# Layers 1 to 3 of a graph network: ring slots freed by counted steps, tile stores issued by ScalarE, words read as 16-bit halves

## The chip, the cores and the metric

The kernel runs on 1 core of one Trainium2 chip. The metric is the device time of one execution in microseconds (us), of the core's whole program. The number to compare against is the median of 3 runs of the kernel before.

## The reference

Four layers of a graph network run over 6250 nodes with 256 features each and 100,000 edges. The edges are sorted by destination node. Each layer ends in `x = layernorm(x + layer(x))`. What matters of it:

```python
edge_index = jnp.stack([src, dst])
x = _layernorm(x + _L0_gnn_ref(x, edge_index, ...))            # attention, 8 heads, softmax over a node's edges
x = _layernorm(x + _L1_gnn_ref(x, edge_index, ...))            # two graph convolutions:
    # msg = h[src] * norm[:, None]; segment_sum(msg, dst) + b;  256 -> 512 -> 256, layer norms and relu
x = _layernorm(x + _L2_gnn_ref(x, edge_weight, W, b, src, dst))
    # msg = hw[src] * sym_norm[:, None]; relu(segment_sum(msg, dst) + b)
x = _layernorm(x + _L3_gnn_ref(x, edge_index, edge_attr_2, ...))  # mixed messages, 4 heads, softmax weights
```

In every layer the costly part is the same: for each edge, fetch the row of its source node, scale it, and add it to the sum of its destination node.

## The kernel before

**Chunks, tiles, steps.** The nodes lie in 49 tiles of 128 (`T = NODE_TILES`), the edges in chunks of 128. A pass over the edges gathers 783 chunks (`POSITIONS`): GpSimd issues one indirect DMA a chunk, which brings 128 rows of 256 numbers from a table in HBM into a slot of a ring in SBUF (`ring_rows`, 60 slots, `SLOTS`). A chunk on the border of two tiles is used for both, so there are 831 steps (`RANKED`), and step i uses chunk i minus the rank of its tile (0 to 48). The rank, the ring slot and the number of chunks that must have landed are data: they are worked out at the start and stored in `step_rows`. `slot_row` has one 32-bit word a step: the slot's offset in the low half, the chunks needed in the high half. `ends_row` has one word a chunk: how many steps must be over before the chunk's slot is free.

**Stages.** A start and layer 0 (with its own loop), then three passes by the class `EdgePass` (line 1372 on): pass 1 and pass 2 are the two convolutions of layer 1 (`edges1`, `edges2`), pass 3 is layer 2 (`edges3`). The change's words count these as "layers 1 to 3". The last stage is layer 3 of the reference, called `mix_...` here and layer 4 in the text. A stage's gathers read a table that the stage before stores tile by tile, so GpSimd begins a pass only when all 49 stores have landed.

**A step of a pass.** TensorE multiplies a one-hot matrix (which edge goes to which node, made by ScalarE in `hots`, or with weights by VectorE in `weighted_hots`) by the gathered rows (`step`, line 1453); VectorE adds the product to the tile's sum in `reg_acc` (`add`, line 1463). When a tile's last step is over, its closing runs spread over the next 16 steps (`closings`, `PARTS`): in pass 1 dense layer, layer norm, second dense layer, at the end ScalarE's scaled copy out of PSUM (line 1533; lines 1670 and 1783 in passes 2 and 3).

**What sets the order.** Each engine's queue is written out by hand, and the engines meet at semaphores:
- GpSimd (`EdgePass.gpsimd`, line 1399) waits ahead of gather j until the product of step j - 12 is made (`AHEAD = SLOTS - (NODE_TILES - 1)` is 12). As step j - 12 uses chunk j - 12 - rank, this is 12 + rank chunks.
- SP (`EdgePass.sync`) waits for the arrival of each chunk in order and counts it on one semaphore, `landed` (line 1414), on which TensorE waits. Between two arrivals, at the chunks that `STORE_AT` names, it waits for a closed tile's copy and issues the store of that tile (line 1410).
- Ahead of pass 2, SP issues the loads of the layer's weights and, by `load_x` (line 463), seven loads of 896 KB that bring `x` back. All of this stands ahead of `EdgePass.sync` in SP's queue.
- TensorE reads the slot words into registers, 16 steps at a time (`load_slots`, line 846), and takes each apart with a mask (line 850) and a shift (in `chunks_needed`). ScalarE and VectorE do the same in layer 4.
- In layer 4 (`mix_gpsimd`, `mix_sync`) GpSimd may be 60 chunks ahead already: SP reads `ends_row` (`load_ends`, line 865), waits until that many steps are over, and signals the slot free (line 1875), 8 chunks early (`FREE_EARLY`).

Of the kernel before, what the change touches and what calls it, by code (L numbers as in the profile page):

```python
# [8 lines left out]
I32 = mybir.dt.int32  # L9
ALU = mybir.AluOpType  # L10
# [6 lines left out]
FEAT = 256  # L17
# [27 lines left out]
AHEAD = SLOTS - (NODE_TILES - 1)  # L45
# [20 lines left out]
STORE_AT = [min(WHOLE[k] + PARTS + 3 - k, POSITIONS) for k in range(T)]  # L66
# [193 lines left out]
def build(nc, io):  # L260
    ctx = ExitStack()
    with ctx:
# [26 lines left out]
        ends_row = step_rows[ROW_OF_ENDS:ROW_OF_ENDS + 1, 0:POSITIONS]  # L289
        group_row = sb("group_row", NODE_TILES, rows=1)  # L290
# [39 lines left out]
        s_landed = [signal(f"pass{k}_landed") for k in (1, 2, 3, 4)]  # L330
        s_free = signal("slot_free")
# [508 lines left out]
        def load_slots(e, name, t0):  # L840

            if name not in slot_regs:
                slot_regs[name] = ([e.alloc_register(f"slot{k}") for k in range(GROUP)],
                                   [e.alloc_register(f"part{k}") for k in range(2)])
            n = min(GROUP, STEPS_PAD - t0)
            e.load(slot_regs[name][0][0:n], slot_row[:, t0:t0 + n])

        def slot_rows(e, name, t, a, b):
            words, parts = slot_regs[name]
            e.reg_alu(parts[0], words[t % GROUP], PLACES - 1, op=ALU.bitwise_and)  # L850
            v = e.snap(parts[0], min_val=0, max_val=(SLOTS - 1) * FEAT)
            return scratch[:, bass.DynSlice(v + a if a else v, b - a)]

        def chunks_needed(e, name, t):
            words, parts = slot_regs[name]
            e.reg_alu(parts[1], words[t % GROUP], 16, op=ALU.logical_shift_right)
            return e.snap(parts[1], min_val=1, max_val=POSITIONS)
# [3 lines left out]
        def load_ends(e, c0, n):  # L861

            if not end_regs:
                end_regs.extend(e.alloc_register(f"end{k}") for k in range(ENDS_AT_ONCE))
            e.load(end_regs[0:n], ends_row[0:1, c0:c0 + n])  # L865
# [511 lines left out]
        class EdgePass:  # L1377
# [6 lines left out]
            def __init__(self, table, weighted, landed, banks):  # L1384
                self.table, self.weighted, self.banks = table, weighted, banks
                self.landed = landed
                self.landed_n = landed.take(POSITIONS)
                self.got = [s_slot[k].take(len(range(k, POSITIONS, ARRIVALS))) for k in range(ARRIVALS)]
                self.product, self.added = s_edge.take(RANKED), s_added.take(RANKED)
                if weighted:  # L1390
                    self.hot = s_hot.take(RANKED)
                else:
                    self.far, self.hot4 = s_far.take(RANKED), s_hot4.take(-(-RANKED // 4))

            def gpsimd(self, e):
                for j in range(POSITIONS):
                    if j >= AHEAD:
                        e.wait_ge(*self.product(j - AHEAD))
                    e.indirect_dma_start(  # L1399
                        ring_rows[:, j % SLOTS, :], None, self.table,  # L1400
                        bass.IndirectOffsetOnAxis(ap=src_idx[:, j:j + 1], axis=0)).then_inc(*self.got[j % ARRIVALS].up)

            def sync(self, e, table, taken, stored, at):


                done = 0
                for j in range(POSITIONS + 1):
                    while done < T and STORE_AT[done] == j:
                        e.wait_ge(*taken(done))
                        e.dma_start(node_rows(table, done, done + 1), at(done)).then_inc(*stored[done % len(stored)].up)  # L1410
                        done += 1
                    if j < POSITIONS:
                        e.wait_ge(*self.got[j % ARRIVALS](j // ARRIVALS))
                        e.sem_inc(*self.landed_n.up)  # L1414
# [60 lines left out]
        edges1 = EdgePass(tab_x1, False, s_landed[0], psum[6:8])  # L1475
# [39 lines left out]
        def pass1_scalar(e):  # L1515
            edges1.hots(e, range(8))
            for i in range(RANKED + PARTS):
                edges1.hots_ahead(e, i)
                for k, n in closings(i):
# [11 lines left out]
                    if n == 16:  # L1531
                        e.wait_ge(*dense2.product(k))
                        e.mul(sums[:, k, :], dense2.out(k), dinv[:, k:k + 1]).then_inc(*taken2.up)

# [30 lines left out]
        def close1_sync(e):  # L1565
            edges1.sync(e, tab_h2, taken2, [h2_stored], lambda k: acc[:, k:k + 1, 0:FEAT])
# [12 lines left out]
        edges2 = EdgePass(tab_h2, False, s_landed[1], psum[4:8])  # L1579
# [13 lines left out]
        def pass2_sync(e):  # L1593
# [9 lines left out]
            edges2.sync(e, tab_x2, taken_l2, x2_stored, lambda k: staged[:, k % 2:k % 2 + 1, :])  # L1603
# [41 lines left out]
        def pass2_scalar(e):  # L1645
            edges2.hots(e, range(8))
            for i in range(RANKED + PARTS):
                edges2.hots_ahead(e, i)
                for k, n in closings(i):
# [16 lines left out]
                    if n == 16:  # L1666
# [3 lines left out]
                        e.copy(staged[:, k % 2, :], dense_l2.out(k)).then_inc(*taken_l2.up)  # L1670

# [64 lines left out]
        edges3 = EdgePass(tab_x2, True, s_landed[2], psum[4:8])  # L1736
# [10 lines left out]
        def pass3_sync(e):  # L1747
            edges3.sync(e, tab_h3, taken_l3, h3_stored, lambda k: staged[:, k % 2:k % 2 + 1, 0:ROW3])
# [12 lines left out]
        def pass3_scalar(e):  # L1761
            for i in range(RANKED + PARTS):
                for k, n in closings(i):
# [15 lines left out]
                    if n == 10:  # L1779
# [3 lines left out]
                        e.copy(staged[:, k % 2, 0:ROW3], dense_l3.out(k)).then_inc(*taken_l3.up)  # L1783

# [459 lines left out]
```

## Time and profile before

| what | value |
|---|---|
| median of 3 runs | 5310.72 us (5306.38 to 5313.35) |
| span of the profiled execution, the only time that is known of it | 5313.9 us |
| pass 1, gathers | from 1236.1 us on |
| pass 2, gathers | 2244.0 to 3235.0 us |
| pass 3, gathers | last start at 4231.2 us |
| layer 4, gathers | 4243.1 to 5223.5 us |
| busy: TensorE, VectorE, ScalarE, GpSimd | 3931.6, 3517.2, 2554.6, 3875.0 us |

How to read it: the busy times are sums over stages with different limits, so the trace is asked stage by stage. In the trace PE is TensorE's matmul and PEld its weight load, DVE is VectorE, ACT is ScalarE, POOL is GpSimd. An engine's name with a q (PEldq, DVEq, SPq) is its sequencer, which runs register instructions, waits and DMA issues. "issue" as a releaser means that the profile shows nothing that the engine waited for. A time with the mark <- names the instruction that ended the idle time ahead of it.

### The profile page before, as it was taken

What the parts mean: (1) busy time and instruction counts of PE and PEld (TensorE: products, weight loads), DVE (VectorE), ACT (ScalarE), POOL (GpSimd) and SP (SyncE); (2) the same over time, 40 slices, a digit from 0 to 9 for tenths busy, and PEclk for the clock granted to TensorE, in tenths of its full rate; (3) what the DMA queues carried; (4) which work ended last, traced back from release to release, by engine and by line L of the source; (5) the groups of instructions that cost most, each with busy time, mean ns of one, the idle gap of its engine ahead of it and who ended that gap; (6) DMA issues with size and microseconds to landing.
All of it is one profiled execution on the core that took longest, in us unless ns stands there. A gap on an engine that the chain in (4) does not pass through costs nothing.

```text
span 5313.9 us, 86764 instructions
## 1 busy us (share of the span) xinstructions
PE 3931.6 (74%) x13357; PEld 2389.2 (45%) x13357; DVE 3517.2 (66%) x10780; ACT 2554.6 (48%) x6938; POOL 3875.0 (73%) x3995
## 2 busy tenths in 40 slices
PE   6888888887777777677777777777677656666763
PEld 4666666664444444344444443343333333444442
DVE  6789888885554545444444445666666578888887
ACT  1667667664555555455545552000000166666665
POOL 3777777775777777677777776777777677777775
PEclk8889889988899998887777777877888777777776
DMA  5444444443333333443333333333333322222222
GB/s 151 113 122 126 122 126 124 120 121 98 111 112 112 111 112 111 118 139 111 111 112 112 111 112 100 109 109 109 109 108 109 98 57 57 57 57 57 57 57 68
DMA packets 252628, 549.14 MB, mean 103 GB/s; under 512 B 71467, under 2 KB 136235, under 8 KB 252108
## 3 DMA queue, kind: packets, MB, share of 16 engines
q0 software_dynamic: 178752, 478.34, 32.8%
q1 hardware_dynamic: 66972, 58.64, 3.5%
q10 hardware_dynamic: 6384, 6.62, 0.5%
q8 instruction: 157, 2.57, 0.2%
q14 instruction: 363, 2.97, 0.2%
HBM read 501.16 MB, written 42.15 MB: 102 GB/s over the span
## 4 chain that ended last, share of the span: by engine, by line
PE 32%; POOL 22%; DMA 18%; issue 13%; DVE 6%; ACT 6%; SPq 2%; DVEq 1%; ACTq 0%; POOLq 0%
PE bank L1453 18%; POOL scratch L1863 12%; DMA scratch<-tab_x,src_idx 10%; POOL scratch L1399 9%; DMA scratch<-tab_h,src_idx 7%; PE bank L1297 4%; PE bank L172 4%; PE bank L1154 3%; DVE reg_acc L1463 2%; ACT scratch L1066 2%; POOL reg_x L1024 2%; SPq L865 1%; DVE reg_acc L1322 1%; PE bank L1142 1%; PE bank L157 1%
## 5 line engine op out<-in xcount | busy, mean ns | idle before, releaser
L1453 PE MATMUL bank<-scratch 128*128 x4986 | 1946.5, 501 | 739.9 <-SPq L1414 356.6
L1463 DVE TENSOR_TENSOR reg_acc<-reg_acc,bank 128x256 f32 x2493 | 1047.3, 420 | 1368.2 <-PE bank L1453 1310.3
L1399 POOL DMA_INDIRECT scratch<-tab_x,src_idx x1566 | 1494.3, 954 | 533.5 <-issue 259.4
L1453 PEld LDWEIGHTS bank<-scratch 128*128 128x128 f32 x4986 | 961.2, 229 | 1630.2 <-issue 1582.6
L1024 POOL DMA_INDIRECT reg_x<-tab_h,src_idx x832 | 838.7, 1008 | 302.7 <-issue 184.1
L1399 POOL DMA_INDIRECT scratch<-tab_h,src_idx x783 | 746.6, 953 | 264.7 <-issue 153.0
L1863 POOL DMA_INDIRECT scratch<-tab_h,src_idx x783 | 743.0, 949 | 249.3 <-issue 226.8
L1916 PE MATMUL bank<-reg_w,scratch 128*128 128x260 f32 x1664 | 639.8, 527 | 282.7 <-issue 180.1
L1423 ACT ACTIVATE scratch<-iota_row,dst_loc 128x128 f32<-128x128 f32 x1662 | 579.6, 393 | 345.5 <-PE bank L1453 336.1
L1297 PE MATMUL bank<-reg_x,scratch 128*128 128x265 f32 x1664 | 582.4, 461 | 72.7 <-DVE reg_x L1339 70.4
L1916 PEld LDWEIGHTS bank<-reg_w,scratch 128*128 128x128 f32 x1664 | 376.3, 252 | 505.1 <-issue 305.0
L1946 ACT ACTIVATE edge_w<-scratch,attr 128x68 f32 x832 | 288.3, 346 | 311.8 <-SPq L1877 282.0
L1297 PEld LDWEIGHTS bank<-reg_x,scratch 128*128 128x128 f32 x1664 | 305.0, 216 | 205.3 <-DVE reg_x L1339 174.5
L1322 DVE TENSOR_TENSOR reg_acc<-reg_acc,bank 128x265 f32 x832 | 353.5, 425 | 34.2 <-PE bank L1297 23.1
L2032 DVE TENSOR_TENSOR reg_acc<-reg_acc,bank 128x260 f32 x832 | 349.2, 420 | 15.7 <-issue 4.2
L1339 DVE TENSOR_TENSOR reg_x<-reg_x 128x256 f32<-128x256 f32 x832 | 342.6, 412 | 0.4 <-ACT reg_x L1107 0.4
L1439 DVE TENSOR_SCALAR scratch<-iota_row,dst_loc,edge_w 128x128 f32<-128x128 f32 x831 | 322.3, 389 | 6.1 <-issue 6.1
L1931 ACT ACTIVATE scratch<-iota_row,dst_loc 128x128 f32<-128x128 f32 x832 | 319.7, 386 | 3.1 <-DMA tab_h<-reg_w 1.6
L1767 ACT ACTIVATE adst<-adst,small 128x1 f32<-128x1 f32 x49 | 14.4, 294 | 617.4 <-DVE adst L1807 617.4
L2015 DVE SCALAR_TENSOR_TENSOR reg_w<-scratch,attr,edge_w 128x68 f32<-128x68 f32 x832 | 236.3, 284 | 99.9 <-ACT edge_w L1946 87.3
L2063 DVE TENSOR_TENSOR reg_w<-reg_w,bank 128x520 f32<-128x520 f32 x416 | 285.6, 686 | 0.4
L1428 ACT ACTIVATE scratch<-scratch 128x512 f32<-128x512 f32 x416 | 261.7, 629 | 13.1
(313 smaller groups left out, 4364.1 us busy)
## 6 DMA issues: line engine op xcount, KB each, us to landing
scratch<-tab_x,src_idx POOLq DMA_INDIRECT x1566, 2.8
scratch<-tab_h,src_idx POOLq DMA_INDIRECT x1566, 2.7
reg_x<-tab_h,src_idx POOLq DMA_INDIRECT x832
tab_h<-scratch ACTq DMA_DIRECT2D x7, 924.0 KB, 5.2
reg_x<-in_x SPq DMA_DIRECT2D x7, 896.0 KB, 11.3
reg_w<-in_x SPq DMA_DIRECT2D x49, 128.0 KB, 2.3
tab_x<-reg_acc SPq DMA_DIRECT2D x49, 128.0 KB
tab_xs<-reg_w SPq DMA_DIRECT2D x49, 128.0 KB, 2.6
```

The lines of the kernel that those rows point to most:

```text
L1024: e.indirect_dma_start(rows0[:, t % (3 * S), 0:ROW0], None, tab_h0, bass.IndirectOffsetOnAxis(ap=src_idx[:, t:t + 1], axis=0)).then_inc(*g ...
L1297: e.matmul(psum[i % BANKS0][:, 0:W0_ROW], hots0[:, i % (2 * S), :], rows0[:, i % (3 * S), :], start=True, stop=True).then_inc(*product0.up)
L1322: e.tensor_tensor(v, v, psum[i % BANKS0][:, 0:W0_ROW], ALU.add).then_inc(*added0.up)
L1339: e.tensor_tensor(v, v, bcast(row[:, FEAT:ROW0], 2, [P, H, D]), ALU.mult).then_inc(*weighted0.up)
L1399: e.indirect_dma_start(ring_rows[:, j % SLOTS, :], None, self.table, bass.IndirectOffsetOnAxis(ap=src_idx[:, j:j + 1], axis=0)).then_inc(* ...
L1423: e.activation(ring_hots[:, i % HOTS, :], iota_row[:, :], ACT.Abs, scale=-1.0, bias=dst_loc[:, i:i + 1]).then_inc(*self.far.up)
L1439: e.tensor_scalar(ring_hots[:, i % HOTS, :], iota_row[:, :], dst_loc[:, i:i + 1], edge_w[:, i:i + 1], ALU.is_equal, ALU.mult).then_inc(*se ...
L1453: e.matmul(self.bank(i), ring_hots[:, i % HOTS, :], rows, start=True, stop=True).then_inc(*self.product.up)
L1463: e.tensor_tensor(v, v, self.bank(i), ALU.add).then_inc(*self.added.up)
L1863: e.indirect_dma_start(ring_rows[:, j % SLOTS, 0:ROW3], None, tab_h3, bass.IndirectOffsetOnAxis(ap=src_idx[:, j:j + 1], axis=0)).then_inc( ...
L1916: e.matmul(psum[i % BANKS][:, 0:WIDE3], hots3[:, i % HOTS, :], scaled3[:, i % 4, :], start=True, stop=True).then_inc(*product3.up)
L2032: e.tensor_tensor(v, v, psum[i % BANKS][:, 0:WIDE3], ALU.add).then_inc(*added3.up)
```

## The change

In the three passes GpSimd's wait for the product of step j - 12 becomes a wait for slot j - 60 to be free, from gather 60 on. SP gives that signal, as it does in layer 4: it loads the counts of `ends_row`, 14 at a time, waits until TensorE has made so many products of this pass (each pass has a product semaphore of its own now, so that the count begins at 0), and counts the slot free. `FREE_EARLY` is 8, so ahead of arrival j SP frees chunk j - 52. The stores of the closed tiles leave SP's queue: ScalarE issues each right behind its own copy, after a wait for that copy to be over. `STORE_AT` goes. The slot words are read as two 16-bit halves each, into 32 registers a group, so the mask and the shift go, on TensorE in the passes and on ScalarE and VectorE in layer 4; the counts of `ends_row` are read as every second half.

```diff
@@ -7,6 +7,7 @@
 I32 = mybir.dt.int32
+U16 = mybir.dt.uint16
 ALU = mybir.AluOpType
@@ -42,7 +43,6 @@
 SLOTS = 60
-AHEAD = SLOTS - (NODE_TILES - 1)
 ARRIVALS = 64
@@ -63,7 +63,6 @@
 PARTS = 16
-STORE_AT = [min(WHOLE[k] + PARTS + 3 - k, POSITIONS) for k in range(T)]
 NI, NF = 4, 3
@@ -287,6 +286,7 @@
         ends_row = step_rows[ROW_OF_ENDS:ROW_OF_ENDS + 1, 0:POSITIONS]
+        slot_halves, end_halves = slot_row.bitcast(U16), ends_row.bitcast(U16)
         group_row = sb("group_row", NODE_TILES, rows=1)
@@ -328,6 +328,7 @@
         s_landed = [signal(f"pass{k}_landed") for k in (1, 2, 3, 4)]
+        s_through = [signal(f"pass{k}_product") for k in (1, 2, 3)]
         s_free = signal("slot_free")
@@ -840,21 +841,16 @@
             if name not in slot_regs:
-                slot_regs[name] = ([e.alloc_register(f"slot{k}") for k in range(GROUP)],
-                                   [e.alloc_register(f"part{k}") for k in range(2)])
+                slot_regs[name] = [e.alloc_register(f"slot{k}") for k in range(2 * GROUP)]
             n = min(GROUP, STEPS_PAD - t0)
-            e.load(slot_regs[name][0][0:n], slot_row[:, t0:t0 + n])
+            e.load(slot_regs[name][0:2 * n], slot_halves[:, 2 * t0:2 * (t0 + n)])
...
         def slot_rows(e, name, t, a, b):
-            words, parts = slot_regs[name]
-            e.reg_alu(parts[0], words[t % GROUP], PLACES - 1, op=ALU.bitwise_and)
-            v = e.snap(parts[0], min_val=0, max_val=(SLOTS - 1) * FEAT)
+            v = e.snap(slot_regs[name][t % GROUP * 2], min_val=0, max_val=(SLOTS - 1) * FEAT)
             return scratch[:, bass.DynSlice(v + a if a else v, b - a)]
...
         def chunks_needed(e, name, t):
-            words, parts = slot_regs[name]
-            e.reg_alu(parts[1], words[t % GROUP], 16, op=ALU.logical_shift_right)
-            return e.snap(parts[1], min_val=1, max_val=POSITIONS)
+            return e.snap(slot_regs[name][t % GROUP * 2 + 1], min_val=1, max_val=POSITIONS)
@@ -862,7 +858,7 @@
                 end_regs.extend(e.alloc_register(f"end{k}") for k in range(ENDS_AT_ONCE))
-            e.load(end_regs[0:n], ends_row[0:1, c0:c0 + n])
+            e.load(end_regs[0:n], end_halves[:, 2 * c0:2 * (c0 + n):2])
@@ -1381,12 +1377,14 @@
-            def __init__(self, table, weighted, landed, banks):
+            def __init__(self, table, weighted, landed, product, banks):
                 self.table, self.weighted, self.banks = table, weighted, banks
...
                 self.got = [s_slot[k].take(len(range(k, POSITIONS, ARRIVALS))) for k in range(ARRIVALS)]
-                self.product, self.added = s_edge.take(RANKED), s_added.take(RANKED)
+                self.product, self.added = product.take(RANKED), s_added.take(RANKED)
+                self.free = s_free.take(POSITIONS - SLOTS)
+                assert self.product.base == 0
                 if weighted:
@@ -1394,24 +1392,23 @@
                 for j in range(POSITIONS):
-                    if j >= AHEAD:
-                        e.wait_ge(*self.product(j - AHEAD))
+                    if j >= SLOTS:
+                        e.wait_ge(*self.free(j - SLOTS))
                     e.indirect_dma_start(
...
-            def sync(self, e, table, taken, stored, at):
-
-
-                done = 0
-                for j in range(POSITIONS + 1):
-                    while done < T and STORE_AT[done] == j:
-                        e.wait_ge(*taken(done))
-                        e.dma_start(node_rows(table, done, done + 1), at(done)).then_inc(*stored[done % len(stored)].up)
-                        done += 1
-                    if j < POSITIONS:
-                        e.wait_ge(*self.got[j % ARRIVALS](j // ARRIVALS))
-                        e.sem_inc(*self.landed_n.up)
+            def sync(self, e):
+
+                for j in range(POSITIONS):
+                    c = j - SLOTS + FREE_EARLY
+                    if inside(c, POSITIONS - SLOTS):
+                        if c % ENDS_AT_ONCE == 0:
+                            load_ends(e, c, min(ENDS_AT_ONCE, POSITIONS - SLOTS - c))
+                        e.wait_ge(self.product.sem, steps_through(e, c))
+                        e.sem_inc(*self.free.up)
+                    e.wait_ge(*self.got[j % ARRIVALS](j // ARRIVALS))
+                    e.sem_inc(*self.landed_n.up)
@@ -1472,7 +1469,7 @@
         loads1 = s_load.take(5)
-        edges1 = EdgePass(tab_x1, False, s_landed[0], psum[6:8])
+        edges1 = EdgePass(tab_x1, False, s_landed[0], s_through[0], psum[6:8])
         hid = reg_x[:, 6 * FEAT:6 * FEAT + 4 * HIDDEN].rearrange("p (s f) -> p s f", s=4)
@@ -1531,6 +1528,8 @@
                         e.mul(sums[:, k, :], dense2.out(k), dinv[:, k:k + 1]).then_inc(*taken2.up)
+                        e.wait_ge(*taken2(k))
+                        e.dma_start(node_rows(tab_h2, k, k + 1), acc[:, k:k + 1, 0:FEAT]).then_inc(*h2_stored.up)
@@ -1563,7 +1562,7 @@
         def close1_sync(e):
-            edges1.sync(e, tab_h2, taken2, [h2_stored], lambda k: acc[:, k:k + 1, 0:FEAT])
+            edges1.sync(e)
@@ -1576,7 +1575,7 @@
         loads2 = s_load.take(8)
-        edges2 = EdgePass(tab_h2, False, s_landed[1], psum[4:8])
+        edges2 = EdgePass(tab_h2, False, s_landed[1], s_through[1], psum[4:8])
         w3_t = t_order.named("attn w00 w01 w10 w11")
@@ -1600,7 +1599,7 @@
             load_x(e, tab_xs, x1_back)
-            edges2.sync(e, tab_x2, taken_l2, x2_stored, lambda k: staged[:, k % 2:k % 2 + 1, :])
+            edges2.sync(e)
@@ -1668,6 +1667,9 @@
                         e.copy(staged[:, k % 2, :], dense_l2.out(k)).then_inc(*taken_l2.up)
+                        e.wait_ge(*taken_l2(k))
+                        e.dma_start(node_rows(tab_x2, k, k + 1),
+                                    staged[:, k % 2:k % 2 + 1, :]).then_inc(*x2_stored[k % 2].up)
@@ -1733,7 +1735,7 @@
-        edges3 = EdgePass(tab_x2, True, s_landed[2], psum[4:8])
+        edges3 = EdgePass(tab_x2, True, s_landed[2], s_through[2], psum[4:8])
         stat3, moment3, root3, inverse3, shift3, scaled3_x = (s.take(T) for s in norm_a)
@@ -1745,7 +1747,7 @@
         def pass3_sync(e):
-            edges3.sync(e, tab_h3, taken_l3, h3_stored, lambda k: staged[:, k % 2:k % 2 + 1, 0:ROW3])
+            edges3.sync(e)
@@ -1781,6 +1783,9 @@
                         e.copy(staged[:, k % 2, 0:ROW3], dense_l3.out(k)).then_inc(*taken_l3.up)
+                        e.wait_ge(*taken_l3(k))
+                        e.dma_start(node_rows(tab_h3, k, k + 1),
+                                    staged[:, k % 2:k % 2 + 1, 0:ROW3]).then_inc(*h3_stored[k % 2].up)
...
```

## Rows read from the trace of the kernel before

**Rows 1.** Source view of line 1399, the gathers of layers 1 to 3: form, durations, idle before.

```profile
L1399 POOL DMA_INDIRECT scratch<-tab_x,src_idx x1566: 942/949/1442, 1236.1 to 4231.2; - x196
L1399 POOL DMA_INDIRECT scratch<-tab_h,src_idx x783: 941/949/1187, 2244.0 to 3235.0; - x196
...
  issue: 412.4, 1353
  PE bank L1453: 309.7, 993
  DMA tab_x<-reg_acc: 43.1, 1
  DMA tab_h<-reg_acc: 19.3, 1
  DMA tab_x<-reg_w: 13.7, 1
```

**Rows 2.** Source view of line 1863, layer 4's gathers.

```profile
L1863 POOL DMA_INDIRECT scratch<-tab_h,src_idx x783: 940/946/1187, 4243.1 to 5223.5; - x196
...
  issue: 226.8, 744
  SPq L1875: 11.6, 38
  DMA tab_h<-reg_w: 11.0, 1
```

**Rows 3.** Windows: pass 1, pass 2, layer 4; busy us (count) per engine, PEclk, DMA share, GB/s.

```profile
1236.00:2243.00 1007.00, 778.93 (x2544) 451.38 (x2544) 500.33 (x1174) 509.07 (x1283) 750.16 (x783) 0.91 0.38 111
2244.00:3249.00 1005.00, 755.38 (x1965) 412.96 (x1965) 477.90 (x1380) 506.78 (x1333) 746.58 (x783) 0.75 0.40 117
...
4243.00:5224.00 981.00, 652.64 (x1763) 389.49 (x1763) 822.71 (x2544) 642.35 (x1946) 742.53 (x783) 0.75 0.25 57
```

**Rows 4.** Timeline of GpSimd: gathers 11 and 12 (from 0) of pass 2.

```profile
2257.74 0.95 POOL L1399 DMA_INDIRECT scratch<-tab_h,src_idx  x1 [0.30 <-issue]
2265.99 0.94 POOL L1399 DMA_INDIRECT scratch<-tab_h,src_idx  x1 [7.31 <-PE bank L1453]
```

**Rows 5.** Chain of waits from pass 1's last store to pass 2's first product.

```profile
2242.03 0.32 SPq L1410
...
2260.90 3.30 SPq L463
...
2264.50 1.64 PE bank L1453 x3
```

**Rows 6.** The same chain further on, where a landing holds it again.

```profile
2282.26 4.21 DMA scratch<-tab_h,src_idx
```

**Rows 7.** Page, DMA issues: count, median us from issue to landing.

```profile
scratch<-tab_h,src_idx POOLq DMA_INDIRECT x1566, 2.7
```

**Rows 8.** Source views of lines 846, 865, 1044 (register loads) and 850 (mask).

```profile
L846 PEldq TENSOR_LOAD <-step_rows x156: 1101/1105/1403, 1245.5 to 4215.3; - x156
L846 DVEq TENSOR_LOAD <-step_rows x52: 1096/1098/1110, 4243.7 to 5209.7; - x52
...
L865 SPq TENSOR_LOAD <-step_rows x52: 1162/1624/2882, 4309.5 to 5204.8; - x52
...
L1044 SPq TENSOR_LOAD <-closed_row x49: 262/267/470, 111.4 to 1194.1; - x49
...
L850 PEldq ALU_OP  x2493: 32/32/42, 1246.7 to 4232.9; - x192
L850 DVEq ALU_OP  x832: 40/40/57, 4244.8 to 5227.0; - x167
```

**Rows 9.** Source view of line 567, the only stores that ScalarE issues.

```profile
L567 ACTq DMA_DIRECT2D tab_h<-scratch x7: 366/366/439, 32.8 to 93.2; - x7
```

**Rows 10.** Timeline at 1314 us in pass 1, VectorE and GpSimd.

```profile
1313.91 0.68 DVE L1563 TENSOR_TENSOR reg_x<-reg_x,reg_w 128x512 f32<-128x512 f32 x1
1314.05 1.36 POOL L1399 DMA_INDIRECT scratch<-tab_x,src_idx  x1 [0.31 <-PE bank L1453]
```

## The prediction

> **What bounds the kernel now.** I first asked which stages the change touches: layers 1 to 3 (three passes over 783 chunks each), and layer 4 where it reads the slot words. Then I asked for the one engine that never rests there. The gather's own view [rows 1] answers it. 1566 and 783 gathers take 949 ns each, and the idle time ahead of them is 412.4 + 309.7 + 43.1 + 19.3 + 13.7 = 798.2 us. Three of these (76.1 us) are the starts of the passes, each behind the last store of the layer before. One is 7.3 us, the longest of the 993 that are put down to TensorE. What is left, 714.8 us over 2345 gathers, is 0.305 us each, and this is the same whether the releaser is named "issue" or "PE bank". So it isn't waiting at all: it is GpSimd's own gap between two gathers. Layer 4 proves it. There GpSimd may already be 60 chunks ahead, and its idle time is 226.8 + 11.6 = 238.4 us over 782 gathers, again 0.305 each [rows 2].
>
> So GpSimd issues without a break at 0.949 + 0.305 = 1.254 us a chunk, 982 us a pass, and everything else fits beneath: of pass 1's 1007 us TensorE is busy 779, VectorE 500, ScalarE 509; pass 2 and layer 4 have the same picture, except that VectorE is busy 823 of layer 4's 981 us [rows 3]. The limit of 12 steps (12 + rank chunks) is met once in three passes.
>
> That one place: in pass 2 gather 12 starts at 2265.99 after 7.31 us idle, while the one before started at 2257.74 [rows 4]. It waits for the product of step 0. The chain shows why that is late [rows 5]: SP issues the layer's loads first, the last of seven tile loads (line 463) ends only at 2264.2, and only then does SP report that chunk 0 has landed; TensorE starts at 2264.50. Thus 7.31 - 0.305 = 7.0 us of GpSimd's time are lost to the short window.
>
> **The change part by part.**
>
> 1. Window of 60. Gather 12 of pass 2 no longer waits, and the first that can wait is gather 60, at 2244 + 60 x 1.254 = 2319, 55 us after TensorE has started. TensorE then finds more chunks at 2264.5 than before, but it drains fast: in the trace it has caught up with the landings by 2282.26 [rows 6], when some 25 chunks had been gathered (12, and 13 more in the 16.3 us from 2265.99), 17.8 / 25 = 0.71 us a chunk against 1.25 arriving. At 2264.5 GpSimd has issued 17 gathers, and one needs 2.7 us to land [rows 7], so about 14 lie ready; TensorE catches up after 14 x 0.71 / (1 - 0.71 / 1.25) = 23 us, long before the pass ends at 3235. What is late next is GpSimd itself, again. Gain **-7.0 us**. Passes 1 and 3 gain nothing: no other long wait stands in their rows.
>
> 2. SP's counted frees. Each pass gets 723 free signals and 52 loads of 14 words (line 865), which cost SP 1.16 to 2.88 us each in layer 4 [rows 8]. Behind such a load up to three landings go unreported, so TensorE starts late by up to 2.9 us. At 0.71 against 1.25 us a chunk it has this back after about 5 chunks. The last load of a pass comes 17 chunks ahead of its end, so the tail is clean. GpSimd waits for the free signal, which is given 8 gathers, 10 us, ahead of need. The same code with the same loads runs in layer 4, where the 38 gathers put down to SP waited 11.6 / 38 = 0.305 us, so not at all. Only the stride is new (every second half-word). Cost 0, and nothing can be gained by it. If the cover went (SP late by more than those 10 us less a landing's 2.7), each time would cost a stall; one load of the longest kind uncovered in each pass is the upper bound I take, 3 x 2.88 = +8.6 us.
>
> 3. Stores by ScalarE. 49 a pass leave SP, where one took 0.32 us [rows 5], and come to ScalarE, where the only measured issue takes 366 ns [rows 9]. That is 49 x 0.366 = 18 us a pass on an engine that idles 498 us of pass 1, and its one-hots are made 8 steps ahead. Behind each waiting issue stand only those one-hots and the next tiles' small steps. The wait on its own copy is one that SP had too. On the path stands only the last store of each pass, since the next pass's gathers start behind it: 3 x (0.366 - 0.32) = **+0.14 us**. SP's loads for pass 2 start 0.3 us earlier, which nothing waits for any more.
>
> 4. Half-words. For every step the mask goes (32 ns on TensorE's queue, 40 ns on VectorE's) and so does the shift; each group of 16 steps loads 32 registers, not 16. One register took 267 ns and sixteen 1.10 us [rows 8], 0.056 us for each more, so 32 are about 1.99 us (estimate from those rows; ends 1.10, if size costs nothing, and 2.2, if it doubles). For VectorE in layer 4 that is 52 x 0.89 = 46 us more and 832 x 0.040 = 33 us less, 13 us net on an engine with room; TensorE in a pass: 46 more, 27 less, hidden under GpSimd in the same way. The last load on VectorE is some 39 steps ahead of layer 4's end, so at most one load's surplus shows there: -0.5 to +1 us, taken as 0. The Trainium skill, "DMA: Bandwidth & Descriptors", section "Latency and other measured facts", gives a `tensor_load` a floor of about 600 ns; the 267 ns row speaks against it. Read as a fixed part it would leave (1.10 - 0.6) / 16 a register and 1.6 us for 32 (an estimate from that page and the row), and the sum would stay the same.
>
> Sum: -7.0 + 0.14 = -6.9 us. The profiled execution's span of 5313.9 becomes 5307.0; it lies 3.2 us above the median of the three runs, so I set the sum against that median: 5310.7 - 6.9 = **5303.8 us**.
>
> **The rivals.**
>
> A, nothing gained. The 7 us stall hangs on how long SP's seven tile loads hold it; the profiled execution may be the only one in which they end after gather 12 is due. Against it: the ending is 7 us late, not a fraction. Or the ring is not the limit it seems. Time 5310.7.
>
> B, more gained. Some gathers of pass 1 are long: one took 1.36 us where it began inside line 1563's 0.68 us operation on VectorE [rows 10]. GpSimd was busy 750.16 us in pass 1, 746.58 in pass 2 and 742.53 in layer 4 [rows 3], so such meetings cost up to 7.6 us in pass 1. If the new rhythm keeps the two apart, the time is 5303.8 - 7.6 = 5296.2. Against it: the order of both queues is the same, and GpSimd ran free of TensorE before as well. The Trainium skill's "SBUF — State Buffer", section "SBUF: two separate sides", says that VectorE and GpSimd share a port pair that one holds for a whole instruction; by it the sum would move only with the number of meetings, and the row agrees that a meeting lengthens the gather.
>
> C, slower: register loads. If a load of 32 half-words costs far more than two of 16 words, VectorE in layer 4 becomes the bound. Its room, with its loads beside no other work, is 981 - 823 - 52 x 2 x 1.10 = 44 us. It decides from (44 + 33) / 52 = 1.5 us above today's 1.10, at 2.6 us a load. At 3.3 us (three times) it costs 52 x 2.2 - 33 - 44 = +37 us: 5303.8 + 37 = 5341. For it: SP's 14 words took up to 2.88 us. Against: none of VectorE's 52 slot loads took over 1.11.
>
> **How the numbers follow.** Forecast 0.67, A 0.12, B 0.13, C 0.08. About 0.2% (10.6 us) is what a measurement of this kernel can tell from no change: below 5300.1 is faster, above 5321.3 slower. B falls below, and of the forecast's case some 0.05, since the three runs alone lie 7 us apart: faster 0.18, same 0.74, slower 0.08. The range reaches from B's 5296 to A's 5310.7 and on to part 2's upper bound, 5303.8 + 8.6 = 5312.4, so 5296 to 5313; C is left out.
>
> **What would show it.** In the changed profile: no wait before gather 12 of pass 2, and a first-to-last gather stretch there of about 984 us (now 991.0, from 2244.0 to 3235.0 [rows 1]); idle time ahead of line 1399's gathers of about 791 us; register loads on TensorE near 2 us; VectorE in layer 4 still with gaps; the last store of each pass issued by ScalarE within 0.1 us of its copy. It is wrong if GpSimd's gap changes from 0.305 us, if it waits for SP's free signals, or if passes 1 or 3 get shorter by over 2 us.

## The result, and the profile after

The changed kernel took **5861.61 us** (median of 4 runs, 5860.33 to 5868.02), beside 5312.03 us for the kernel before on the same chip (4 runs, 5306.38 to 5318.47): a ratio of 1.104 (95% interval 1.1024 to 1.1055), +550 us. The forecast was 5303.8 us with a range of 5296 to 5313: wrong, and on the side of rival C. The span of the profiled execution is 5858.5 us, where the one before had 5313.9.

First the term that the forecast took as 0, the register loads. Source views of lines 846 and 861, the loads of slot words and of counts (to be set beside [rows 8]):

```profile
L846 PEldq TENSOR_LOAD <-step_rows x156: 7516/7532/7952, 1239.3 to 4537.6; - x156
L846 DVEq TENSOR_LOAD <-step_rows x52: 7103/7109/7135, 4564.8 to 5748.7; - x52
L846 ACTq TENSOR_LOAD <-step_rows x52: 6668/6692/6863, 4567.2 to 5745.2; - x52
L861 SPq TENSOR_LOAD <-step_rows x208: 1851/2855/3228, 1297.2 to 5667.9; - x104
```

A load of 32 half-words takes TensorE 7.53 us, not the forecast's 1.99: 6.43 us more than the load before, 52 times a pass. Now the stages. Source views of the gathers (lines 1397 and 1868), which answer to [rows 1, 2]:

```profile
L1397 POOL DMA_INDIRECT scratch<-tab_x,src_idx x1566: 940/946/1459, 1230.4 to 4543.2; - x196
L1397 POOL DMA_INDIRECT scratch<-tab_h,src_idx x783: 940/946/1175, 2515.6 to 3498.2; - x196
...
  issue: 613.3, 1997
  SPq L1409: 287.4, 349
  DMA tab_h<-reg_acc: 111.7, 1
  DMA tab_x<-reg_w: 64.3, 1
  DMA tab_x<-reg_acc: 39.9, 1
```

```profile
L1868 POOL DMA_INDIRECT scratch<-tab_h,src_idx x783: 938/944/1192, 4564.3 to 5681.0; - x196
...
  SPq L1880: 192.9, 182
  issue: 183.8, 600
```

One gather costs what it did. Of the 287.4 and 192.9 us put down to SP's free signal, 0.305 us each time is GpSimd's own gap; 181 and 137 us are true waiting. In the passes, all of it lies in pass 1: in passes 2 and 3 the waits for SP are 61 and 67, none over 0.3 us. New too are the starts: pass 2 began 111.7 us after pass 1's last gather had ended, not 19.3. Stage by stage, from a stage's first gather to that of the next (for layer 4 to the end of the span):

| stage | before | after | more | first to last gather, before | after |
|---|---|---|---|---|---|
| pass 1 | 1007.9 | 1285.2 | +277 | 987.6 | 1172.6 |
| pass 2 | 1005.7 | 1047.9 | +42 | 991.0 | 982.6 |
| pass 3 | 993.4 | 1000.8 | +7 | 981.5 | 979.8 |
| layer 4 | 1070.8 | 1294.2 | +223 | 980.4 | 1116.7 |

With a start of pass 1 that was 5.7 us earlier they make up the difference of the spans. Two stages pay nearly all, and for different engines. In passes 2 and 3 the gathers run as before and what is lost lies behind the last one: TensorE is behind by then, and the next pass starts 64.3 us after pass 2's last gather, not 13.7. Windows of the four stages, columns as in [rows 3]:

```profile
1230.00:2515.00 1285.00, 804.45 (x2544) 476.67 (x2544) 496.65 (x1174) 510.08 (x1284) 749.32 (x783) 0.83 0.30 87
2516.00:3563.00 1047.00, 601.13 (x1965) 419.76 (x1965) 465.20 (x1380) 489.19 (x1332) 744.93 (x783) 0.78 0.38 112
3564.00:4564.00 1000.00, 586.42 (x1956) 416.35 (x1956) 588.73 (x1905) 89.94 (x245) 741.95 (x783) 0.76 0.37 107
4564.00:5858.00 1294.00, 683.13 (x1825) 416.38 (x1825) 879.15 (x2729) 653.07 (x2035) 777.11 (x790) 0.71 0.20 48
```

Register instructions don't count as busy. In layer 4 the slot loads are 52 x 7.11 = 370 us on VectorE, beside 57 us for its loads of ranks; part of each load runs under operations issued before it. Added up over the trace, VectorE stands still for 339 us within its loads (before: 37), so with 879 us busy 1218 of 1294 us are taken. ScalarE comes to 653 + 317 = 970. That makes VectorE the bound there, by this sum; no run gave the two engines' loads back one at a time. In pass 1 TensorE stands still for 338 us within its slot loads, and 804 + 338 = 1142 of 1285 us are taken. In passes 2 and 3 it stands still just as long, 345 and 336 us, but is busy for 601 and 586 us only, and GpSimd's 980 us cover nearly all of it.

Busy time isn't a fixed amount of work. In pass 2 the same 1965 matmuls took TensorE 755 us before and 601 now, when it works through what has gathered behind each load. In pass 1 it was 779 and became 804.

Of the waits, three lines name the loads:

```profile
PE bank L1450 <- issue: 565.3, 288, 7.5
DVE reg_w L2020 <- issue: 310.6, 48, 6.8
ACT edge_w L1951 <- issue: 248.4, 42, 6.6
```

"issue" says that the profile shows nothing the engine waited for, and the longest of these are about as long as one load. Before, the three were 46.0, 10.2 and 7.1 us, none of them longer than 0.9 us. The chain of waits in pass 1 shows what it looks like on the path:

```profile
1700.55 0.64 ACT scratch L1425
1701.19 3.96 issue
1705.14 3.19 PE bank L1450 x6
...
1725.02 5.03 issue
1730.05 3.88 PE bank L1450 x8
```

Every 20-odd us there is such a hole. No wait names its cause, so a reader of the waits alone would blame SP or the landings. The timeline of TensorE's own matmuls and the windows around the first hole (columns as in [rows 3]) show what stands behind it:

```profile
1705.14 1.22 PE L1450 MATMUL bank<-scratch 128*128 x2 [5.96 <-issue]
...
1697.00:1699.00 2.00, 2.00 (x11) 1.58 (x9) 0.10 (x1) 0.47 (x1) 1.70 (x2) 1.00 0.39 111
...
1705.00:1707.00 2.00, 1.85 (x4) 1.17 (x4) 0.42 (x1) 0.00 (x0) 0.33 (x1) 0.50 0.00 0
1707.00:1709.00 2.00, 2.00 (x7) 1.50 (x6) 0.84 (x2) 0.20 (x1) 1.55 (x2) 0.50 0.23 66
```

TensorE stood still for 5.96 us. Its granted clock was 1.00 ahead of that and 0.50 (the lower level, 1.2 GHz) for some 4 us behind it, so it makes up for the hole slowly at first. Over pass 1 the granted clock fell from 0.91 [rows 3] to 0.83, and the busy time rose by 25.5 us for the same 2544 matmuls. How much of the 277 us is due to the clock was not tried.

### The profile page after: what moved, and what is told of

The parts are those of the page before. It is cut to its first block, busy times and chain, and to the rows that moved or that the text cites. A ratio compares the mean times of both kernels' runs of the same rounds, so it can differ in the third digit from the quotient of the medians.

```text
span 5858.5 us, 87101 instructions
## 1 busy us (share of the span) xinstructions
PE 3683.5 (63%) x13357; PEld 2470.3 (42%) x13357; DVE 3439.8 (59%) x10780; ACT 2508.7 (43%) x6938; POOL 3867.4 (66%) x3995
## 4 chain that ended last, share of the span: by engine, by line
PE 23%; issue 23%; POOL 22%; DVE 8%; ACT 8%; DMA 8%; SPq 6%; DVEq 2%; ACTq 0%; POOLq 0%
POOL scratch L1397 19%; PE bank L1450 7%; SPq L861 5%; PE bank L1293 4%; PE bank L171 4%; DMA scratch<-tab_x,src_idx 4%; DMA scratch<-tab_h,src_idx 3%; PE bank L1921 3%; PE bank L1150 2%; POOL scratch L1868 2%; ACT scratch L1062 2%; DVE reg_acc L2037 1%; POOL reg_x L1020 1%; DVE reg_w L2020 1%; DVE reg_w L2068 1%
## 5 line engine op out<-in xcount | busy, mean ns | idle before, releaser
L1450 PE MATMUL bank<-scratch 128*128 x4986 | 1667.9, 472 | 1208.0 <-SPq L1411 620.9
L1450 PEld LDWEIGHTS bank<-scratch 128*128 128x128 f32 x4986 | 1047.4, 231 | 1738.3 <-issue 1604.2
L1868 POOL DMA_INDIRECT scratch<-tab_h,src_idx x783 | 740.9, 946 | 396.8 <-SPq L1880 192.9
L1420 ACT ACTIVATE scratch<-iota_row,dst_loc 128x128 f32<-128x128 f32 x1662 | 556.3, 391 | 370.1 <-PE bank L1450 358.2
L1936 ACT ACTIVATE scratch<-iota_row,dst_loc 128x128 f32<-128x128 f32 x832 | 320.8, 387 | 8.6 <-PE bank L1921 3.0
L1436 DVE TENSOR_SCALAR scratch<-iota_row,dst_loc,edge_w 128x128 f32<-128x128 f32 x831 | 303.9, 367 | 6.1 <-issue 6.1
```

The lines of the kernel that those rows point to most:

```text
L1420: e.activation(ring_hots[:, i % HOTS, :], iota_row[:, :], ACT.Abs, scale=-1.0, bias=dst_loc[:, i:i + 1]).then_inc(*self.far.up)
L1450: e.matmul(self.bank(i), ring_hots[:, i % HOTS, :], rows, start=True, stop=True).then_inc(*self.product.up)
L1868: e.indirect_dma_start(ring_rows[:, j % SLOTS, 0:ROW3], None, tab_h3, bass.IndirectOffsetOnAxis(ap=src_idx[:, j:j + 1], axis=0)).then_inc( ...
```

## The experiments

**Chips.** The experiments were run in four sets. In three of them the kernel before took 6563 to 6626 us in place of 5310 (the last section has more on this). Every ratio is therefore to the kernel before on the chip of the same set. Where 32-bit words are read in what follows, each loaded value that a wait uses has one mask more than in the kernel before, to keep it within 16 bits ("bounded"); its price is measured by itself.

**1. Which part is it?** words_back: the change whole, but slots and counts read as 32-bit words again.

```diff
-            e.load(slot_regs[name][0:2 * n], slot_halves[:, 2 * t0:2 * (t0 + n)])
+            e.load(slot_regs[name][0][0:n], slot_row[:, t0:t0 + n])
...
-            e.load(end_regs[0:n], end_halves[:, 2 * c0:2 * (c0 + n):2])
+            e.load(end_regs[0:n], ends_row[0:1, c0:c0 + n])
```

> The changed kernel, but slot words and counts are read as 32-bit words again, with mask and shift (and one more mask a wait, so that no wait's value can be negative). Theory L (the loads of 32 half-words cost it all): slot loads fall from 7.5 to 1.1 us, GpSimd is unbroken again, and the time is the forecast's, 5304 us (5298 to 5313). Theory F (SP's counted frees and ScalarE's stores cost it): the time stays over 5700 us and GpSimd still waits for SP in pass 1.

halves_alone: the kernel before with nothing but the half-word slot loads.

> The kernel before, with half-words in the slot loads and nothing else of the change (the counts keep words). Theory L: as slow as the changed kernel or a little slower, since the window of 12 now stops GpSimd whenever TensorE falls behind: 5850 to 6000 us. Theory F: 5312 us, no change.

Measured on the slow chip: before 6562.85; words_back 6690.82, ratio 1.0197 (1.0178 to 1.0215); halves_alone 7201.04, ratio 1.0983 (1.0959 to 1.1006). The whole change, in another set as changed_again, has 1.0922. So the half-words of the slot loads alone make all of the loss, and without half-words it is gone but for 2%: theory L. The absolute times expected were those of a faster chip. A second run of the same kernel, words_again, gave 1.0207 (1.0187 to 1.0228):

> The same kernel as in the run words_back (32-bit words everywhere, with the new window, SP's frees and ScalarE's stores), once more, since that run met a chip on which the kernel before took 6563 us and many register instructions took 700 ns in place of 30 to 110. Theory L: on a chip that runs the kernel before in 5312 us, 5304 us and no register instruction over 300 ns. Theory F: over 5400 us there too, since SP has 2000 more instructions in its queue.

**2. Where the 2% are from.** words_bounded is the kernel before plus the extra mask, nothing else; changed_again is the changed kernel, for the same chip.

```diff
-            return e.snap(parts[1], min_val=1, max_val=POSITIONS)
+            e.reg_alu(parts[2], parts[1], PLACES - 1, op=ALU.bitwise_and)
+            return e.snap(parts[2], min_val=1, max_val=POSITIONS)
```

> The kernel before with one more mask ahead of each wait whose value was loaded (one register instruction a step on TensorE, and on ScalarE in layer 4; one a chunk on SP), nothing else. It is the control for words_back, which has it too. Theory L: on a fast chip no difference, 5312 us; on a slow one it is this and not SP's frees that made words_back 2% slower: 1.02 times before. Theory F: no difference on either, within 0.3%.

> The changed kernel itself, for comparison with the other runs of this chip. On a chip that runs the kernel before in 5312 us: 5861 us. On a chip like that of the last runs (kernel before at 6560 to 6630 us): theory L expects the same surplus as the half-words alone brought there, 1.10 times the kernel before.

changed_again: 7232.38, ratio 1.0922 (1.0899 to 1.0944). words_bounded: 6758.84, ratio 1.0219 (1.0197 to 1.0240). The mask alone costs the whole 2% there, and SP's frees and ScalarE's stores add nothing that can be seen. (On the faster chip the mask costs nothing: see 6.)

**3. The price of a load by itself.** load_probe2: ScalarE in pass 3, where it has little to do, makes extra loads of fourteen forms into unused registers, and a wait that always holds uses the last one. An earlier form of it, load_probe (6685.28 us, one run), had loads that nothing used, and its trace contains none of them; it showed nothing of their price.

> Loads into spare registers in ScalarE's queue in pass 3, where it is busy 9% of the time: 1, 2, 4, 8, 16, 32 words; 1, 2, 4, 8, 16, 32 half-words; 14 every second half; 14 words; each used once by a wait that is over. If the cost goes by 16-bit element: 16 half-words 3.4 us, 32 half-words 6.7, 32 words 2.0 to 2.2. If it is the number of registers over 16 that costs: 32 words 6.7 us as well, and 16 half-words 1.0. The kernel's time stays within 0.2% of the kernel before.

Its one run took 6782.57 us, 2.4% over the kernel before and not within 0.2%; it has the extra mask too, which costs 2.2% there. The durations of single loads are what it was for. Source views, ScalarE's register loads: 1, 4, 16, 32 words; 1, 4, 16, 32 half-words; 14 half-words, every second one; 14 words (durations ns min/median/max).

```profile
L1776 ACTq TENSOR_LOAD <-step_rows x10: 285/289/295, 4234.9 to 5206.5; - x10
L1780 ACTq TENSOR_LOAD <-step_rows x9: 312/316/321, 4254.7 to 5114.5; - x9
L1784 ACTq TENSOR_LOAD <-step_rows x9: 1014/1022/1040, 4272.3 to 5132.9; - x9
L1786 ACTq TENSOR_LOAD <-step_rows x9: 1956/1970/2085, 4281.0 to 5141.4; - x9
L1788 ACTq TENSOR_LOAD <-step_rows x9: 272/274/278, 4283.3 to 5143.7; - x9
L1792 ACTq TENSOR_LOAD <-step_rows x9: 886/893/984, 4299.8 to 5160.5; - x9
L1796 ACTq TENSOR_LOAD <-step_rows x9: 3389/3402/3439, 4307.9 to 5170.5; - x9
L1798 ACTq TENSOR_LOAD <-step_rows x9: 6755/6765/6803, 4323.2 to 5184.4; - x9
L1800 ACTq TENSOR_LOAD <-step_rows x10: 2977/3000/3212, 4229.8 to 5193.6; - x10
L1802 ACTq TENSOR_LOAD <-step_rows x10: 1232/1240/1257, 4233.3 to 5196.9; - x10
```

Half-words: (6.765 - 0.274) / 31 = 0.21 us each, one by one, with and without the stride of two. Words: (1.970 - 0.316) / 7 = 0.236 us for each four. 32 words cost what 32 registers were forecast to cost (1.97 against 1.99 us); it is the element's type that costs, by a factor of 3.4. So of the two expectations the first holds: the cost goes by the 16-bit element, not by registers over 16.

**4. Which engine pays where.** halves_on_tensor: the change, with half-words on TensorE alone.

```diff
-            e.load(slot_regs[name][0:2 * n], slot_halves[:, 2 * t0:2 * (t0 + n)])
+            if name == "tensor":
+                e.load(slot_regs[name][0][0:2 * n], slot_halves[:, 2 * t0:2 * (t0 + n)])
+            else:
+                e.load(slot_regs[name][0][0:n], slot_row[:, t0:t0 + n])
```

> The changed kernel with 32-bit slot words on ScalarE and VectorE (layer 4), half-words on TensorE alone. Theory L: the three passes stay as in the changed kernel (1285, 1048, 1001 us) and layer 4 with its end goes back from 1294 to 1071 us: 5861 - 223 = 5638 us.

two_banks: the changed kernel, pass 2 with two PSUM banks for its products, as pass 1 has, not four.

```diff
-        edges2 = EdgePass(tab_h2, False, s_landed[1], s_through[1], psum[4:8])
+        edges2 = EdgePass(tab_h2, False, s_landed[1], s_through[1], psum[6:8])
```

> The changed kernel, pass 2 with two PSUM banks for its products, as pass 1 has, in place of four. If it is the two banks that keep TensorE in pass 1 from catching up after a load (each product waits for VectorE's sum of two steps before), pass 2 goes from 1048 us to about 1200 and the kernel to 6010 us. If it is pass 1's heavier closings, pass 2 stays at 1048 and the kernel at 5861.

Both ran on one slow chip (before 6625.50), changed_again in another set (before 6616.41). The three passes, in which halves_on_tensor and changed_again are the same, differ by 6 to 10 us (0.4 to 0.7%), so that much is noise between the sets. halves_on_tensor: ratio 1.0677 (1.0647 to 1.0706) where the whole change has 1.0922. Its layer 4 lasts 1437.3 us from the first gather on, that of changed_again 1591.8: 154 us come back from VectorE and ScalarE alone. With words everywhere it lasts 1405.0 on the same chip (words_again), so most of layer 4's loss is these two engines' loads. two_banks: 1.1076 (1.1043 to 1.1109). The gathers of pass 2 in changed_again and in two_banks (source views of line 1397):

```profile
L1397 POOL DMA_INDIRECT scratch<-tab_h,src_idx x783: 941/949/1205, 3048.8 to 4260.4; - x196
```

```profile
L1397 POOL DMA_INDIRECT scratch<-tab_h,src_idx x783: 943/949/1202, 3039.2 to 4327.0; - x196
```

1211.6 us became 1287.8, and to pass 3's first gather it is 87 us more (77 against halves_on_tensor on the same chip). The loads stop TensorE as long as before (336 us in pass 2, and 324 with four banks); what grew is its busy time, from 661 to 753 us, so with two banks it is slower in making up for the holes. The outcome lies between the two expected, some 150 us and nothing. Pass 1 took 1498 us there, 204 more than pass 2, so two banks account for 77 to 87 of these. Two banks with cheap loads were not run, so it is not shown that the banks cost this only together with the loads. Pass 1's closings, which put two dense layers between the steps, are the other difference, and were not tried.

**5. SP's and the window's parts.** end_halves: words_back with only the counts read as every second half-word.

> The changed kernel with 32-bit slot words, but the counts for SP still read as every second half. Theory L: SP's loads take 2.9 us in place of 1.6, which the 8 gathers of lead cover: the same time as with words everywhere, within 3 us, 5304 us. Theory F: slower than with words by over 10 us, with GpSimd waiting for SP.

words_16: words_back with 16 counts a load, not 14.

```diff
-ENDS_AT_ONCE = 14
+ENDS_AT_ONCE = 16
```

> 32-bit words everywhere, and the counts for SP loaded 16 at a time in place of 14. The probe had 16 words in 1.02 us (four at a time) and 14 in 1.24, and 14 from an address that is not a multiple of 16 bytes may go one by one, in 2.9 us. Expected: SP's loads all at 1.1 to 1.2 us; time 5304 us on a fast chip, as words_back on a slow one or up to 0.5% less.

loads_between: words_bounded, with SP's seven tile loads of pass 2 each behind the fourth next arrival, not all ahead of the first.

> The kernel before (bounded as in words_bounded), with its old window of 12 and SP's stores, but pass 2's seven tile loads go out one by one between the first arrivals (after arrival 1, 5, 9 and so on). If gather 12 waited only for them, the 7 us stall goes without any larger window: 7 us less than words_bounded, 5305 us on a fast chip.

end_halves: 1.041 (1.0388 to 1.0432), 2.1% above words_back and not the same time as expected, on a chip where slow instructions sit on SP as well. On that chip the half-word counts do cost something of their own. words_16: 1.0160 (1.0137 to 1.0182), below words_bounded's 1.0219. loads_between: 1.0214 (1.0193 to 1.0236), no different from it. In its profile the wait of 8.0 us at gather 12 is gone, but one of 4.8 us stands at gather 18 in its place, and 7 us couldn't be seen among that chip's runs. This left the question of the forecast's own part open, until a set of runs met a chip like the first.

**6. The dose, and the forecast's own part.** Four kernels, on a chip where the kernel before took 5310.16 us (27 runs). half_dose is words_16, in which TensorE reads of every 16 steps 8 as words and 8 as half-words:

```diff
+            if name == "tensor":
+                e.load(slot_regs[name][0][0:8], slot_row[:, t0:t0 + 8])
+                e.load(slot_regs[name][0][8:24], slot_halves[:, 2 * t0 + 16:2 * t0 + 32])
```

> The kernel of words_16, but of each group of 16 steps TensorE reads the first 8 as words (0.55 us) and the last 8 as 16 half-words (3.4 to 3.8 us): about 4.3 us a group in place of 1.1, half of the changed kernel's surplus. If each us of a load costs from the first one on, the three passes lose half of what they lose with 32 half-words. If it costs only past TensorE's idle time (228 us in pass 1, 250 and more in passes 2 and 3, that is 4.4 us a group), they lose little: pass 1 within 40 us of words_16 on the same chip, passes 2 and 3 within 20.

> The kernel of words_16, beside its control on one chip. Window, SP's frees and ScalarE's stores together are worth 7 us (0.13%) by the forecast on a chip without the 700 ns stalls. On a chip with them, by words_16 and words_bounded of the last runs, 0.6% less than the control.

stores_alone: words_bounded, with each tile's store moved from SP to ScalarE as in the change.

> The kernel of words_bounded with the tile stores issued by ScalarE, and nothing else. Forecast's part 3: +0.14 us, so no difference to words_bounded, within 0.2%.

> The control on the same chip: the kernel before with the extra mask. 5312 us on a fast chip, 1.02 times the kernel before on one with 700 ns stalls.

| kernel | us | ratio to before (95%) |
|---|---|---|
| bounded_again | 5307.80 | 0.9994 (0.9985 to 1.0003) |
| stores_alone | 5310.34 | 0.9999 (0.9990 to 1.0008) |
| words_16_again | 5304.34 | 0.9984 (0.9975 to 0.9993) |
| half_dose | 5436.12 | 1.0232 (1.0216 to 1.0248) |

words_16_again is the rest of the change with cheap loads (mask and shift stay, and SP reads 16 counts at a time), and **it lands at 5304.3 us**, on the forecast's 5303.8. By the medians it is 3.5 us below bounded_again, 6.0 below stores_alone and 5.8 below the kernel before: a small gain, near the limit of what these runs can tell. Gather 12 of pass 2 in bounded_again and in stores_alone (timeline of GpSimd), still late as in [rows 4]:

```profile
2270.73 0.94 POOL L1402 DMA_INDIRECT scratch<-tab_h,src_idx  x1 [7.51 <-PE bank L1456]
```

```profile
2264.34 0.94 POOL L1402 DMA_INDIRECT scratch<-tab_h,src_idx  x1 [5.45 <-PE bank L1452]
```

In words_16_again it isn't late:

```profile
2264.87 0.95 POOL L1405 DMA_INDIRECT scratch<-tab_h,src_idx  x1 [0.30 <-issue]
```

Its source views:

```profile
L1405 POOL DMA_INDIRECT scratch<-tab_h,src_idx x783: 942/946/1197, 2249.9 to 3231.6; - x196
...
  issue: 689.3, 2263
...
  SPq L1417: 25.3, 83
...
L847 PEldq TENSOR_LOAD <-step_rows x156: 1101/1106/1600, 1249.6 to 4211.1; - x156
...
L868 SPq TENSOR_LOAD <-step_rows x184: 679/972/1171, 1307.5 to 5205.9; - x184
```

2249.9 to 3231.6 is 981.7 us, against 991.0 [rows 1]. The waits for SP are 25.3 / 83 = 0.305 us each, GpSimd's own gap. In half_dose the two loads of a group cost 0.59 + 3.80 us (source views of lines 848 and 849), 3.28 us more than words:

```profile
L848 PEldq TENSOR_LOAD <-step_rows x156: 587/591/875, 1244.9 to 4336.8; - x156
L849 PEldq TENSOR_LOAD <-step_rows x156: 3787/3795/4120, 1245.5 to 4337.5; - x156
```

```profile
L1414 POOL DMA_INDIRECT scratch<-tab_x,src_idx x1566: 940/946/1487, 1236.3 to 4352.5; - x196
L1414 POOL DMA_INDIRECT scratch<-tab_h,src_idx x783: 942/946/1202, 2375.8 to 3357.2; - x196
```

Pass 2 is free here: 981.4 us, as with words. Pass 1 is not: 2375.8 - 1236.3 = 1139.5 us to pass 2's first gather, 130 more than words_16_again's 1009.1. So neither expectation held: pass 1 pays about half of its full loss, as if every us counted, and passes 2 and 3 pay nothing. Dose and cost, in us a pass (the middle column against words_16_again, the right one the changed kernel against the kernel before; against words_16_again it would be +276, +51, +9):

| pass | 52 x 3.28 = 171 more | 52 x 6.43 = 334 more |
|---|---|---|
| 1 | +130 | +277 |
| 2 | 0 | +42 |
| 3 | 0 | +7 |

Pass 1 pays about 80% of either dose. 334 us could not have fitted into the 228 us that TensorE idled of its 1007 [rows 3], but 171 could, and cost 130 all the same. Passes 2 and 3 have a threshold between the two doses. The two doses differ in more than the loads: the changed kernel reads SP's counts as half-words too, and has no mask and shift.

## Why the prediction was wrong

- **What bounds the kernel** held as long as the loads are cheap: the median gap between gathers is 0.305 us in every stage of every run. In the changed kernel's pass 1 and layer 4 TensorE and VectorE took its place.
- **Part 1, the window, -7.0 us**, came true in pass 2, whose gathers took 982.6 us in the changed kernel and 981.7 in words_16_again (forecast 984; before 991.0, bounded_again 989.1). The wait stayed where the window stayed, 7.51 and 5.45 us. In the kernel's whole time the gain is seen less well: 3.5 to 6.0 us by the medians above.
- **Part 2, counted frees, 0**, held with word loads: 0.305 us a wait. It held in passes 2 and 3 of the changed kernel too, with loads of 2.86 us for the counts. In its pass 1 and layer 4 GpSimd did wait some 318 us for SP, but SP counts finished steps, and halves_alone, whose passes have no such signal, loses as much. That half-words for the counts cost something of their own was seen on the slow chip alone.
- **Part 3, ScalarE's stores, +0.14 us**: stores_alone is 2.5 us (0.05%) above bounded_again, within the noise of both. No cost is seen; a term of 0.14 us is too small to be shown.
- **Part 4 is the step that failed.** It put a load of 32 half-words at 1.99 us, with ends 1.10 and 2.2. Measured: 7.53 us on TensorE, 7.11 on VectorE, 6.69 on ScalarE. The term counted registers, and the trace before had no load of half-words at all. The upper end, twice 16 words, was no bound: it took the rate of one form for another's. One row spoke for more: SP's loads of 14 words took up to 2.88 us, where 16 words took 1.10 [rows 8]. Rival C noted it and let VectorE's rows outweigh it, but why 14 words can cost more than 16 was never asked. The saving was under-counted too. A source view of line 851 before has 112 ns a step on TensorE for the shift's group, beside the mask's 32, and what is left of both in the changed kernel (line 849) is 38. So a pass saves 831 x 0.106 = 88 us of TensorE's queue and not 27, and pass 1 still got slower by 277.
- **Rival C** had the mechanism for layer 4: VectorE becomes the bound from 2.6 us a load. With the measured load its own sum is 52 x 6.0 - 33 - 44 = +235 us; layer 4 cost +223. It got a chance of 0.08 and a price of +37. That the two numbers are so close is in part luck, as its sum takes no load to run under other work, and leaves out the 36 ns a step of the shift.
- **What neither had** is pass 1's TensorE, +277 us, half of the loss. The prediction hid its loads "under GpSimd in the same way" and gave VectorE a threshold, but TensorE none. Its own rows had one: 228 us idle in pass 1, that is 4.4 us a load, and the loads grew by 6.43. Even below that the room was there as a sum and not in place, as half_dose shows. A load stops the sequencer for 7.5 us at once, and TensorE stands still for 6.85 us of it (median) in pass 1 as in passes 2 and 3; what differs is how fast it makes up for that. Two banks in place of four account for 77 to 87 of the 204 us between passes 1 and 2 on the slow chip; that the rest is the closings is argued, and the share of the lower clock is open.
- Summed with what was measured: 277.3 + 42.2 + 7.4 + 223.4 - 5.7 = 544.6 us, which is 5858.5 - 5313.9. The window's gain of some 7 us is inside pass 2's 42. Why pass 1 starts 5.7 us earlier was not looked into.

## What to carry to other kernels

Ask for the row of the very form: a register load of another element type or alignment can have another price, and if the trace doesn't hold it, price it as elements one by one from the worst row (SP's 14 words in 2.88 us would have given 32 x 0.206 = 6.6 us). An operation that stops a sequencer for microseconds is not hidden by the engine's idle share. First compare its whole dose with the idle time of the stage; then ask how fast the engine can make up for one such stop where it falls, and try a half dose. When several edits come together, a kernel with all but the one is worth its run: here the rest of the change was a small gain.

## What the runs showed of the hardware

- **Register loads.** Half-words come one at a time at 0.21 us, words four at a time at 0.236 us. That holds only where the load starts at a multiple of 16 bytes from the row's begin. Of SP's 52 loads in the kernel before, every second one does: these 26 took 1.16 to 1.37 us, and 25 of the others 2.87 to 2.88, which is 0.206 us a word, one by one (the last has 9 words and took 1.88). With 16 words a load all start so, and those of layer 4 took 0.97 to 0.98 us in words_16_again, but for the short last one. The Trainium skill, "DMA: Bandwidth & Descriptors", section "Latency and other measured facts", states a floor of about 600 ns for a `tensor_load`; 289 ns for one word and 316 ns for four in load_probe2 disagree, and the measurement decides.
- **TensorE's clock behind a stop.** Where a load held TensorE still for 5.96 us, the granted clock was 1.00 ahead of the stop and 0.50 in the 4 us behind it. Over pass 1 it was 0.91 before, 0.87 in half_dose and 0.83 with the whole dose.
- **A slower chip, or a slower time of one.** In three sets of runs the kernel before took 6563 to 6626 us. There register and semaphore instructions that elsewhere take 32 or 17 ns take 0.7 us now and then, and up to 1.4, on several engines (in words_bounded 422 of TensorE's 4986 masks took over 0.3 us, half of them 0.70 or more; before, on the first chip, none). Source views in words_bounded:

```profile
L850 PEldq ALU_OP  x2493: 2/32/1403, 1546.6 to 5333.3; - x192
...
L1417 SPq EVENT_SEMAPHORE  x2349: 1/17/1407, 1541.7 to 5318.1; - x196
```

  The median is the same and the longest is 1.4 us, where the kernel before had 42 and 17 ns on the first chip. There one more mask a wait costs 2.2%, and on the faster chip nothing (0.9994). What causes it stays open.
